# The four projections of an attention block as three fp32r products each, with the queues of a batch in a new order

## The reference

```
x = layernorm(src) * (1 + scale) + shift          # scale, shift from the time step, one pair per batch
q, k, v = x @ Wq + bq, x @ Wk + bk, x @ Wv + bv   # three of the four projections
scores = q k^T / 4 + attention_bias               # a bias of its own for every batch and head
probs = softmax(where(mask, -inf, scores))
x = x + ((probs @ v) @ Wo + bo)                   # the fourth projection
h = layernorm(x) * g2 + beta2
x = x + gelu2(h @ W1 + b1) @ W2 + b2              # width 1024 in between
# then a second block: x is pooled per batch, a small gate gives a strength, and
# strength * (x @ M + c) is added, where M comes from U and V made orthogonal by Gram-Schmidt (32 steps)
```

## Time and profile before

| what | value |
|---|---|
| median of three runs | 1390.7 us |
| profiled execution, its own time | 1390.32 us |
| its span | 1388.2 us |
| stage 1 | to about 893 us |
| PE, DVE, ACT, POOL busy over the span | 96%, 77%, 78%, 63% |
| granted TensorE clock, mean | 0.989 of full speed |
| HBM traffic | 157.63 MB read, 16.78 MB written |

### The profile page before, as it was taken

How to read it: one execution, slowest core, us unless ns; L and a number is a source line. 1 busy time by engine, 2 the same in 40 slices (tenths; PEclk the granted TensorE clock), 3 DMA queues, 4 the chain that set the end, 5 groups by cost and what they waited for, 6 DMA issues and landing times. The chain is left out here.

```text
span 1388.2 us, 39650 instructions
## 1 busy us (share of the span) xinstructions
PE 1335.7 (96%) x11998; PEld 1126.6 (81%) x11998; DVE 1066.6 (77%) x3539; ACT 1077.6 (78%) x2696; POOL 870.3 (63%) x874
## 2 busy tenths in 40 slices
PE   3899999999999999999999998799999999999997
PEld 3677777777777777777777776499999999999997
DVE  3787787777777877887777777577888888787875
ACT  0788888888888888888888887677777777777773
POOL 3989989999999998998998997222122122222210
PEclk9999999999999999999999999989999999999999
DMA  7656555565565564564654671001111111101000
GB/s 229 211 165 200 170 185 188 167 197 177 168 206 167 176 208 155 189 202 150 200 192 154 223 225 33 26 29 32 45 30 32 44 30 38 37 30 45 30 24 32
DMA packets 182766, 175.01 MB, mean 126 GB/s; under 512 B 15648, under 2 KB 182208, under 8 KB 182720
## 3 DMA queue, kind: packets, MB, share of 16 engines
q1 hardware_dynamic: 182720, 174.42, 39.5%
HBM read 157.63 MB, written 16.78 MB: 126 GB/s over the span
## 5 line engine op out<-in xcount | busy, mean ns | idle before, releaser
L423 POOL TENSOR_TENSOR ring<-ring,maskv 128x1024 f32<-128x1024 f32 x256 | 600.0, 2371 | 14.9 <-DMA ring<-in_fside 7.6
L885 ACT ACTIVATE ring<-ring,nmax 128x256 f32<-128x256 f32 x1024 | 453.0, 502 | 28.4 <-DVE nmax L599 28.4
L599 DVE CUSTOM_DVE_ANT_0 ring<-bank,ring 128x256 f32<-128x256 f32 x1024 | 373.1, 418 | 91.2 <-PE bank L1150 74.9
L890 ACT ACTIVATE pT<-bank 128x512 f32<-128x512 f32 x416 | 239.5, 592 | 101.6 <-PE bank L1165 101.5
L1165 PE MATMUL bank<-ident,ring 128*128 128x128 f32 x2048 | 293.5, 279 | 1.4 <-ACT pT L890 1.1
L1165 PEld LDWEIGHTS bank<-ident,ring 128*128 128x128 f32 x2048 | 232.3, 143 | 70.7 <-issue 47.8
L1020 ACT ACTIVATE work<-bank,b1t 128x256 f32<-128x256 f32 x256 | 107.5, 475 | 117.7 <-PE bank L1361 117.7
L1361 PE MATMUL bank<-hT_high,w_high 128*128 128x256 f32 x512 | 154.4, 302 | 4.2 <-DVE hT_rest L771 4.2
L1150 PE MATMUL bank<-work 32*128 32x256 f32 x2048 | 148.3, 404 | 5.2 <-DVE nmax L599 5.2
L1374 PE MATMUL bank<-w_high,gT_high 128*128 128x256 f32 x512 | 148.1, 289 | 0.0
L455 POOL TENSOR_SCALAR vpeb<-mvb 128x2 f32<-128x2 f32 x32 | 6.1, 191 | 226.5 <-DVE mvb L686 226.2
(11 more groups left out here) (158 smaller groups left out, 2724.3 us busy)
## 6 DMA issues: line engine op xcount, KB each, us to landing
ring<-in_fside SPq DMA_DIRECT2D x128, 1024.0 KB, 7.5
xt<-in_x SPq DMA_DIRECT2D x32, 256.0 KB, 3.1
x_d<-x2s SPq DMA_DIRECT2D x32, 256.0 KB, 7.7
work<-x_d SPq DMA_DIRECT2D x32, 256.0 KB, 2.7
out<-pT SPq DMA_DIRECT2D x32, 256.0 KB, 2.2
mk<-in_mask SPq DMA_DIRECT2D x32, 64.0 KB, 6.5
w<-in_W SPq DMA_DIRECT2D x2, 1024.0 KB, 10.5
wada<-in_W_ada SPq DMA_DIRECT2D x1, 512.0 KB, 4.3
```

The source lines that it names most:

```text
L423: nc.gpsimd.tensor_tensor(v, v, m, ALU.add).then_inc(s_masked, 1)
L599: nc.vector.tensor_tensor_reduce(out=v, in0=score_ps[h % HG][:, qt], in1=v, scale=-1.0, scalar=ROW_MAX_NEG, op0=ALU.add, op1=ALU.min, accu ...
L885: nc.scalar.activation(v, v, ACT.Exp, bias=nmax[:, b.par, h, qt:qt + 1], scale=-1.0).then_inc(s_exp, 1)
L890: nc.scalar.activation(pT[:, h % (2 * HG)], tp_ps[h % 2], ACT.Copy).then_inc(s_pta, 1)
```

## The change

The weights Wq, Wk, Wv and Wo are split once, at the start, into a high part (ACT, four copies) and a rest (DVE, four subtractions). The new semaphore waits put these ahead of the first batch. In every batch `xT` and the transposed context are split too: `xT_high` and `ctxT_high` on ACT (the second is the copy that was there, now into fp32r) and `xT_rest` and `ctxT_rest` on DVE. `xT_rest` reads two tensors in SBUF; `ctxT_rest` reads one in PSUM and one in SBUF. Each projection becomes twelve fp32r matmuls where there were four float32 ones, and the projections of q, k and v wait for the rest of `xT`, that of the context for its rest. To make room, the unsplit weights lie in `pT`, and some small tiles of the setup lie in others.

The order of the batch is also changed on PE, DVE and ACT; SP's and POOL's are as they were. The core of the diff:

```diff
+            def xT_rest(b):
+                dve.wait_ge(s_xh, b.n + 1)
+                if b.i is not None or b.off >= 1:
+                    dve.wait_ge(s_vp, b.n)
+                nc.vector.tensor_tensor(xTs[1][:], xT[:], f32(xTs[0][:]), ALU.subtract).then_inc(s_xl, 1)
+            def ctxT_rest(b):
+                dve.wait_ge(s_ctxT, b.n + 1)
+                nc.vector.tensor_tensor(ctxTs[1][:], tail_ps, f32(ctxTs[0][:]), ALU.subtract).then_inc(s_cl, 1)
...
+            for i in range(4):
+                weight_rest(i)
             nc.vector.memset(pooled[:], 0.0).then_inc(s_setup, 1)
...
+            def xT_high(b):
+                act.wait_ge(s_xT, b.n + 1)
+                if b.i is not None or b.off >= 1:
+                    act.wait_ge(s_vp, b.n)
+                nc.scalar.activation(xTs[0][:], xT[:], ACT.Copy).then_inc(s_xh, 1)
...
             def project_qk(b, t):
-                w = wqp if t == 0 else wkp
+                ws = wqs if t == 0 else wks
                 if t == 0:
-                    pe.wait_ge(s_xT, b.n + 1)
+                    pe.wait_ge(s_xl, b.n + 1)
...
-                        ins = mm(prep_ps[:, n], w[:, c, n * P:(n + 1) * P], xT[:, c], start=(c == 0), stop=(c == DC - 1))
+                        for k, (kw, kx) in enumerate(HI_LO):
+                            ins = mm(prep_ps[:, n], ws[kw][:, c, n * P:(n + 1) * P], xTs[kx][:, c],
+                                     start=(c == 0 and k == 0), stop=(c == DC - 1 and k == len(HI_LO) - 1))
...
             def project_o(b, main):
-                pe.wait_ge(s_ctxT, b.n + 1)
+                pe.wait_ge(s_cl, b.n + 1)
```

More of the change, by code:

```diff
@@ L147, in attention_block_kernel @@
         pT = sb("pT", [P, 2 * HG, QT, S])
+        raw = [pT[:, 2 * (i // 2):2 * (i // 2) + 2].rearrange("p h t s -> p (h t s)")[:, (i % 2) * DC * D:(i % 2 + 1) * DC * D].rearrange("p (c n) -> p c n", c=DC)
+               for i in range(6)]
+        wq, wk, wv, wo, wqp, wkp = raw
+        wada = pT[:, 6:8].rearrange("p h t s -> p (h t s)").rearrange("p (c n) -> p c n", c=2)
         work = sb("work", [P, 8192])
+        turns, red2 = [work[:, i * 2 * B:(i + 1) * 2 * B].rearrange("p (a b) -> p a b", a=2) for i in range(2)]
         qm = work[:, 0:2048].rearrange("p (b a c s) -> p b a c s", b=2, a=2, c=DC)
@@ L658, in prep_all @@
                 xT_out(b)
+                xT_rest(b)
                 q_out(b, 0)
@@ L711, in body @@
                     xT_out(b.plus(1))
+                    xT_rest(b.plus(1))
                 if main:
-                    reduce_head(b, 4)
+                    reduces(b, (4, 5, 6))
+                if prep:
+                    q_out(b.plus(1), 0)
+                if main:
+                    reduce_head(b, 7)
                 if tail:
@@ L918, in gs_write @@
                 nc.scalar.activation(column(i), qcol[:], ACT.Copy).then_inc(s_gself, 1)
+            for i, ((high, rest), w) in enumerate(((wqs, wqp), (wks, wkp), (wvs, wv), (wos, wo))):
+                if i < 2:
+                    act.wait_ge(s_wp, i + 1)
+                if i == 2:
+                    act.wait_ge(s_load_att, 16 * len(loads_att))
+                nc.scalar.activation(high[:], w, ACT.Copy).then_inc(s_wh, 1)
             act.wait_ge(s_setup, 1)
@@ L1214, in project_v @@
                     for c in range(DC):
-                        ins = mm(prep_ps[:, t], xT[:, c, t * P:(t + 1) * P], wv[:, c], start=(c == 0), stop=(c == DC - 1))
+                        for k, (kx, kw) in enumerate(HI_LO):
+                            ins = mm(prep_ps[:, t], xTs[kx][:, c, t * P:(t + 1) * P], wvs[kw][:, c],
+                                     start=(c == 0 and k == 0), stop=(c == DC - 1 and k == len(HI_LO) - 1))
                 ins.then_inc(s_vp, 1)
@@ L1251, in project_o @@
                     for c in range(DC):
-                        ins = mm(tail_ps[:, t], ctxT[:, c, t * P:(t + 1) * P], wo[:, c], start=(c == 0), stop=(c == DC - 1))
+                        for k, (kx, kw) in enumerate(HI_LO):
+                            ins = mm(tail_ps[:, t], ctxTs[kx][:, c, t * P:(t + 1) * P], wos[kw][:, c],
+                                     start=(c == 0 and k == 0), stop=(c == DC - 1 and k == len(HI_LO) - 1))
                 ins.then_inc(s_o, 1)
@@ L1294, in body @@
                 if main:
+                    transposes(b, 3)
+                    transposes(b, 4)
                     scores(b, 2)
@@ L1297, in body @@
                     ctx_natural(b.plus(-1), 1)
+                if main:
+                    transposes(b, 5)
                 if prep:
@@ L1312, in body @@
                 if main:
+                    transposes(b, 8)
+                    transposes(b, 9)
                     gs_gram(b, n)
@@ L1329, in body @@
                 if main:
-                    transposes(b, 14)
+                    transposes(b, 13)
                 if prep:
@@ L1333, in body @@
                 if main:
+                    transposes(b, 14)
+                    pv(b, 2)
                     transposes(b, 15)
-                    pv(b, 2)
                 if n == B:
```

163 lines of the change are left out of this document (85 added, 78 removed).

## The result

The change made the kernel slower. The changed kernel takes 1397.36 us (median; 1396.71 to 1400.17), the kernel before 1390.85 us beside it: a ratio of 1.0053, with an interval of 1.0038 to 1.0068. I had forecast 1384.0. The profiled execution took 1400.17 us, with a span of 1398.0; the other three took 1396.71 to 1397.87, so what the trace shows of it contains some 3 us that belong to this execution and not to the change.

What follows compares the result with a forecast made beforehand. PE's queue bounded stage 1 at 26.29 us a batch, with POOL nearly as full. 1390.3 - 8.4 (steady batches) + 2.4 (start) - 0.3 (last project_o) = 1384.0 us; forecast 1377 to 1391, overall range 1360 to 1398.

Steps and rivals of the forecast that it cites:

- the ring: Stage 1's steady batches: POOL's 15.83 to its adds, two adds 4.68, then 5.50 to coefficients; 26.0 us a batch, 8.4 gained.
- the start: Before and in the first batch: weight splits 2.5, first xT_high and xT_rest 1.3, less 0.8 and 0.6; 2.4 us lost.
- the end: Last two bodies of stage 1: project_o saves 0.3 us once; the new ctxT_rest's 0.6 is taken back.
- the second rival: Stage 1's ring is 0.2 to 0.3 us longer, by late ACT work or PE waits; 1389 to 1398 us, chance 0.20.
- The price at the port: In each batch xT_rest, with two SBUF inputs, waits for POOL's mask add: 0 to 2.34 us possible, mean 1.2 to 1.6 long.
- Twelve take 1.42 us: Each projection on PE: twelve fp32r matmuls take 1.42 us against 1.73, 0.31 less each, 1.24 per batch.
- PE's own side: PE's queue in a stage 1 batch without the port: work of 24.75 us plus waits, 25.2 us.
- 2 x 0.15 = 0.3: PE's new order in a batch: five blocks of small tiles instead of seven, saving 0.3 us.
- k and v, warm, save 0.3 each: First batch: the projections of k and v, at the upper clock level, save 0.3 us each, 0.6 together.
- The first two and the last two bodies I cost at nothing: Loop bodies at stage 1's start and end: no cost or gain per body, except project_o's 0.3 us.
- The first, no price at the port: Rival: xT_rest does not wait or POOL is not held; POOL's 25.26 us a batch decides, 1362 us, chance 0.20.
- The third, three adds: Rival: xT_rest misses the second mask add's end and waits for the third's; 28.35 us a batch, 1453 us, chance 0.10.

Runs made afterwards that it cites:

- Experiment 1: The changed kernel with xT_rest reading its first input from the PSUM bank instead of xT in SBUF (output not the reference's): 1367.79 us, ratio 0.9844.
- experiment 4: The kernel before, with float32 projections, in the new order of the batch on PE, DVE and ACT: 1399.37 us, ratio 1.0064.
- experiment 9: The changed kernel with DVE's preparation of stage 2's constants moved behind copy_pT of head 7 in batch 30: 1392.97 us, ratio 1.0008.
- experiment 6: The changed kernel with xT written back to PSUM and split there, and x_back as two fp32r products with the identity: 1380.84 us, ratio 0.9930.

## Why the prediction was wrong

The forecast was a gain of 6.7 us, and the change costs 6.5. The mechanism of the steady state was right and three sizes were off, all to one side: the ring by 6.4 us (-2.0 for -8.4), the start by 4.8 and the end by 2.7. The time fell where the second rival had put it (the ring 0.2 to 0.3 longer, 1389 to 1398), for other reasons than that rival named: it has the ring but neither the start nor the end.

**The price at the port: right.** xT_rest was forecast at 1.2 to 1.6 us, ending 0.56 behind a mask add; it took 1489 ns in the median (1525 in the mean) and ended 0.55 behind, and the add that it holds up took 2.86 us, forecast 2.9. PE's wait ahead of project_q was to be about 1 and was 0.86. One reading under it was wrong. The mask add of 3340 ns, taken for POOL held up by the two-input add of the earlier trace rows, began at 843.90 and ran beside L668, which scales `w` in SBUF; the two-input add began only as it ended. Experiment 1 shows that the port is the cause, and what the kernel would be without it: 1367.8 us.

**The ring: 26.21, not 26.0.** This is the term that took most of the gain, 28 x 0.21 = 5.9 us (26.23 by the mean of the batches). Step by step against the prediction's 5.50: rest 0.55 (0.56), hand-over 0.05 (0.05), project_q 1.53 (1.42), then 0.63 to the first copy on ACT, two copies 420.83 - 419.86 = 0.97, exponential 0.80, coefficients 1.07 (together 3.47, forecast 3.47). So project_q is 0.11 too long, and gprod to the four adds gave 15.92 for 15.83, the two adds 4.69 for 4.68. The 0.09 is spread over POOL's instructions and has no cause shown. The failed step is "Twelve take 1.42 us": the earlier trace rows are eleven in the middle of a stretch of the same kind, and here the first of twelve, behind another kind of matmul, is 0.23 ahead of the second. In experiment 1 k and o take 1.50 each, without any wait before them. The rate was read from rows without the entry. I had counted such an entry for small tiles and not for this.

**PE's own side: 25.45, not 25.2.** Four entries at some 0.1 make 0.3 to 0.4, and experiment 4 shows that the order's "2 x 0.15 = 0.3" saved was more than taken back (+0.2). Against the 26.50 of experiment 4 the products save 0.30, 0.23, 0.33 and 0.23 for q, k, v and o, which leaves 25.4. PE was not the bound, so this cost nothing in the changed kernel. Without the port PE waits 0.16 us and POOL 0.18 in the batch that I read, so neither is far from being the bound.

**The start: +7.2, not +2.4.** Batch 0 did what the sum says for the weights (xT_out of batch 0 comes 2.34 later for the forecast 2.5). Of the gains set against it, "k and v, warm, save 0.3 each" failed for k: its matmuls are 0.213 us apart, and it takes 2.7 us where it took 1.9. The failed step is "The first two and the last two bodies I cost at nothing": before the ring has found its phase, the rest of batch 1 meets an add 0.9 us after its start and that of batch 2 meets one at its beginning, and they take 2.02 and 2.89 us. Without the port batch 3 is only 1.2 us late (experiment 1). Part of the 7.2 is the clock behind these waits: from batch 2 to 3 the changed kernel took 29.05 us with 0.65 granted from 76 to 80 us, and experiment 9, the same code there and the same wait, took 27.53 with 1.00. Neither bound of mine, 0.5 and 4, held it.

**The end: +2.4, not -0.3.** The same sentence fails a second time. The order puts a copy that PE waits for behind 7.1 us of DVE work that occurs once (847.97 to 855.05), and I had costed only the steady body. Before, PE waited 4.61 us behind the same work, and now 5.62, and it then ran for 8.2 us at the lower level of its clock, where it had been some 3.5. Experiment 9 gives 2.1 of it back in the trace.

**The rivals.** The first, no price at the port, is refuted by the duration of xT_rest, and experiment 1 shows what it would have given: 1367.8 for the forecast 1362. The third, three adds, shows in single batches alone (the maximum of 2891 ns), not in the steady state.

## What to carry to other kernels

Keep an instruction with two SBUF inputs on DVE off a path that GpSimd also closes, where one input can come from PSUM: here such a ring set the period, and the change gave 0.07 us a batch where it gave 0.84 without the port. Check what an order is worth apart from what it orders; here the two depended on each other so much that the order's sign changed. Read a rate for a group with its first member in it, and walk the first three and the last two bodies of a loop by themselves, since what I had costed at nothing there was worth 7.5 us. When an edit moves a wait, look at the clock behind it too: at the end of stage 1 the wait grew by 1.0 us and the slow stretch behind it cost 2.3 more.

## What I had not expected of the hardware

An fp32r matmul with 128 columns started 0.11 us after the one before, as a float32 transpose of 128 does, and one with 256 columns 0.118: so at 128 columns one fp32r matmul was no faster than one float32 transpose in experiment 6, and the two that replace each of them took twice the time. No run tries a size between.

At batch 0 the matmuls of project_q are 0.213 us apart and those in the steady state 0.118. I take these for the two levels of the clock, 1.2 and 2.4 GHz: at 901.50 to 904.00 us of the same execution the distance is 0.213 as well, and the granted clock 0.50. In the profiled execution of the changed kernel k was still at the lower level and v at the upper; in that of experiment 9 all three were at the lower, as in the rows here (the last two of v), and the first scores came 1.8 us later (39.62 for 37.81).

```profile
37.10 0.41 PE L1271 MATMUL bank<-wv_rest,xT_high 128*128 128x256 f32 x1
37.32 0.41 PE L1271 MATMUL bank<-wv_high,xT_rest 128*128 128x256 f32 x1
```

The stretch from 30 to 40 us has a granted clock of 1.00 in both executions all the same, so there the distance of the matmuls and the clock's row do not agree. By batch 31 the two executions are 0.13 us apart (833.70 and 833.83), although batch 3 was 1.04 apart (99.49 and 100.53).
